# Low parts of x and xT of batches 1 to 7: subtracted on GpSimd instead of on the Vector engine

## The chip, the cores and the metric

One core of one Trainium2 chip runs the whole program. The metric is the device time of one execution in microseconds (us). Engines are named as the profile names them: PE is TensorE, DVE is VectorE, ACT is ScalarE, POOL is GpSimd, SP is SyncE, which here only issues DMAs.

## What is computed

Eight graphs (batches) of 1024 nodes with 256 features go through two graph layers, each with a residual and a layer norm:

```python
def layer0(x, adj, W):
    deg = jnp.sum(adj, axis=-1, keepdims=True)
    agg = jnp.einsum('bij,bjf->bif', adj, x) / jnp.maximum(deg, 1e-6)
    return relu(jnp.einsum('bnf,of->bno', jnp.concatenate([x, agg], axis=2), W))

def layer1(x, adj, k, bias):
    Ah = adj + eye
    dh = rsqrt(jnp.sum(Ah, axis=-1))
    An = dh[:, :, None] * Ah * dh[:, None, :]
    return relu(jnp.einsum('bnm,bmf,fc->bnc', An, x, k) + bias)

x = layernorm(x + layer0(x, adj, W))      # x: (8, 1024, 256), adj: (8, 1024, 1024)
x = layernorm(x + layer1(x, adj, k, bias))
```

## The kernel before

All values are float32. Before TensorE uses a matrix, the matrix is split in two: its high part is the value rounded to the matmul's format (`fp32r`), made by ACT with a copy, and its low part is the value minus the high part, made by DVE with a subtraction (`minus`, L443). A product is then three matmuls (L688 to L690): high by high, high by low, low by high. This holds for x (`x_hi`, `x_lo`), for its transpose, used in the projection of layer 0 (`xt_hi`, `xt_lo`), for the adjacency (`a_hi`, `a_lo`, tiles `adj_hi` and `adj_lo` in the profile), for the weights and for every intermediate that is multiplied again (`gath_hi`, `gath_lo`, `x1s_hi`, `x1s_lo`).

There is no scheduler. Each engine has its own program, written by hand and synchronised by counting semaphores, and batches 1 to 6 run in a loop on each engine. In the loop turn of batch b, PE does the second half of the adjacency-times-x product of b (`gather_second`), the projections of layer 0, the propagation of layer 1 (`propagate`), the projection of layer 1 (`project1`), and between those already the first half of the product of batch b+1 (`gather_first`). PE goes through one batch in this order:

- `propagate` for half 0 fills PSUM banks 0 and 1 of `ring_b`. ACT copies each bank to `gath_hi` and DVE makes `gath_lo` of it (`read_g`, numbers 0 and 1).
- `project1` for tiles 0 to 3 waits for `g_lo_done` of these two (L815), then come the rest of `propagate` and, from L820, `gather_first(b + 1, range(TH))`, which needs the first low parts of the new adjacency and of the new x.
- `project1` for tiles 4 to 7 waits for `g_lo_done` of `read_g` 2 and 3 (L821). Then `gather_first(b + 1, range(TH, T))` needs the second half of `x_lo`.
- `gather_second(b + 1, 0)` follows, then `project_x` for tiles 0 to 3, the first reader of `xt_lo` (L789); tiles 4 to 7 read its second piece (L796).

DVE's order in the same stretch (L600 to L625) is: the two halves of `x_lo` of b+1 (`split_x`), the two pieces of `xt_lo` of b+1 (`split_xt`), `read_g` 0 and 1, two chunks of `adj_lo`, `read_g` 2, two more chunks of `adj_lo`, `add_identity`, layer 1's bias, ReLU, residual and statistics (`add_layer1(b, 0)`), and only then `read_g` 3. ACT works through the matching list (L374 to L391), one step ahead of DVE.

POOL makes the identity matrix at the start and is idle afterwards. SP issues the load of the next batch's xT once `xt_lo_done` says that the present one has been split (L237); its next entry in the queue is the store of the first half of the output.

Batch 0's own splits are made in an opening section by DVE (L656 to L675, and L576 for one piece of xT).

Of the kernel before, what the change touches and what calls it, by code (L numbers as in the profile page):

```python
# [4 lines left out]
F32 = mybir.dt.float32  # L5
F32R = mybir.dt.float32r
ALU = mybir.AluOpType
# [3 lines left out]
B, N, F = 8, 1024, 256  # L11
T = N // P
FT = F // P
H = 2
# [6 lines left out]
XP = 2  # L21
# [8 lines left out]
def gnn_two_layers(nc, adjT, adjN, x, xT, w, k, bias, out):  # L30
# [8 lines left out]
    with ctx:  # L39
        def sb(name, shape, dt=F32, align=32):  # L40
            return ctx.enter_context(nc.sbuf_tensor(name, shape, dt, align_bytes=align))

        def sem(name):
            return ctx.enter_context(nc.semaphore(name))
# [4 lines left out]
        x_hi = sb("x_hi", [P, T, F], F32R, LINE)  # L49
        x_lo = sb("x_lo", [P, T, F], F32R, LINE)  # L50
        xt_hi = sb("xt_hi", [P, T, FT, P], F32R, LINE)
        xt_lo = sb("xt_lo", [P, T, FT, P], F32R, LINE)
# [4 lines left out]
        x_sb = sb("x_sb", [P, T, F])  # L57
        xt_raw = sb("xt_raw", [P, T, FT, P])
# [50 lines left out]
        x_hi_done, x_lo_done = sem("x_hi_done"), sem("x_lo_done")  # L109
        xt_hi_done, xt_lo_done = sem("xt_hi_done"), sem("xt_lo_done")  # L110
# [24 lines left out]
        def xt_pieces(t, first, end):  # L135
            return t[:, first * T // XP:end * T // XP, :, :].rearrange("p t f c -> p (t f c)")
# [7 lines left out]
        def x_half(t, h):  # L144
            return t[:, h * TH:(h + 1) * TH, :]
# [112 lines left out]
        def _(pool):  # L258
# [3 lines left out]
                                    fill=1.0, base=0, pattern=[[-1, P]],  # L262
                                    channel_multiplier=1).then_inc(ident_done, 1)

        @block.scalar
        def _(act):
            def copy(o, i):
# [174 lines left out]
        def _(dve):  # L442
            def minus(o, a, hi):  # L443
                return nc.vector.tensor_tensor(o, a, hi.bitcast(F32), ALU.subtract)  # L444
# [8 lines left out]
                                        ident[:, :, :].to_broadcast([P, TH, P]),  # L453
                                        ALU.add).then_inc(diag_ready, 1)

            def split_x(n, h):
                dve.wait_ge(x_hi_done, n * H + h + 1)
                minus(x_half(x_lo, h), x_half(x_sb, h), x_half(x_hi, h)).then_inc(x_lo_done, 1)

            def split_xt(n, i):  # L460
                dve.wait_ge(xt_hi_done, n * XP + i + 1)
                minus(xt_pieces(xt_lo, i, i + 1), xt_pieces(xt_raw, i, i + 1),
                      xt_pieces(xt_hi, i, i + 1)).then_inc(xt_lo_done, 1)

            def read_agg(b, n):
                dve.wait_ge(agg_hi_done, b * 4 + n + 1)
                minus(gath(gath_lo, n), ring_b[:, n, :], gath(gath_hi, n)).then_inc(agg_lo_done, 1)

            def read_g(b, n):
                dve.wait_ge(g_hi_done, b * 4 + n + 1)  # L470
                minus(gath(gath_lo, n), ring_b[:, n, :], gath(gath_hi, n)).then_inc(g_lo_done, 1)
# [6 lines left out]
            def inverse_degrees(b, h):  # L478
                half = b * H + h + 1
                dve.wait_ge(deg_done, b * T + TH * (h + 1))  # L480
                nc.vector.tensor_scalar(deg_c[:], deg[:, h * TH:(h + 1) * TH], DEG_EPS, None,
                                        ALU.max).then_inc(deg_clamped, 1)
                nc.vector.tensor_scalar(v[:, 0:TH], deg[:, h * TH:(h + 1) * TH], 1.0, None,
                                        ALU.add).then_inc(deg_read, 1)
                dve.wait_ge(deg_clamped, half)
                nc.vector.reciprocal(rdeg[:], deg_c[:]).then_inc(rdeg_done, 1)  # L486

            def add_layer0(b, h, pairs=range(0, TH, 2)):
                for q in pairs:
                    t = h * TH + q  # L490
                    for o in range(2):
                        dve.wait_ge(proj0_scaled, b * T + t + o + 1)
                        nc.vector.tensor_tensor(x1[:, t + o, :], ring_a[:, (t + o) % NB, 0:F],  # L493
                                                x1[:, t + o, :], ALU.add).then_inc(proj0_read, 1)
                    dve.wait_ge(proj0_read, b * T + t + 2)
                    nc.vector.scalar_tensor_tensor(
                        x1[:, t:t + 2, :], x1[:, t:t + 2, :], 0.0, x_sb[:, t:t + 2, :],
                        ALU.max, ALU.add).then_inc(resid0_done, 1)
                    dve.wait_ge(resid0_done, b * (T // 2) + t // 2 + 1)
                    for o in range(2):  # L500
                        last = nc.vector.bn_stats(stats[:, q + o, :], x1[:, t + o, :])
                    if q == TH - 2:
                        last.then_inc(stats_done, 1)
# [26 lines left out]
            def variances(b, step, at):  # L530
                n = b * 4 + step + 1
                even_mean, even_cv, odd_mean, odd_cv = (stats[:, :, i] for i in (1, 2, 4, 5))
                dve.wait_ge(stats_done, n)
                nc.vector.tensor_tensor(dmean[:], even_mean, odd_mean, ALU.subtract).then_inc(dmean_done, 1)
                nc.vector.tensor_tensor(smean[:], even_mean, odd_mean, ALU.add)
                nc.vector.scalar_tensor_tensor(cv[:], even_cv, F * LN_EPS, odd_cv, ALU.add, ALU.add)
                dve.wait_ge(dmean_done, n)
                nc.vector.scalar_tensor_tensor(dmean2[:], dmean[:], 0.25, dmean[:],
                                               ALU.mult, ALU.mult).then_inc(dmean2_done, 1)
                dve.wait_ge(dmean2_done, n)  # L540
                nc.vector.scalar_tensor_tensor(v[:, at:at + TH], cv[:], 1.0 / F, dmean2[:],  # L541
                                               ALU.mult, ALU.add).then_inc(var_ready, 1)
# [16 lines left out]
            def lower_x1s(b, h, tiles=range(TH)):  # L559
                for q in tiles:  # L560
                    t = h * TH + q
                    dve.wait_ge(x1s_hi_done, b * T + t + 1)
                    nc.vector.scalar_tensor_tensor(  # L563
                        x1s_lo[:, t, :], x1[:, t, :], dh[:, h, q:q + 1],
                        x1s_hi[:, t, :].bitcast(F32), ALU.mult, ALU.subtract).then_inc(x1s_lo_done, 1)
# [6 lines left out]
            def batch(b, more, first=False):  # L572
                inverse_degrees(b, 0)
                if first:
                    add_layer0(b, 0, [0])
                    split_xt(0, 1)  # L576
                    read_agg(b, 2)
                    add_layer0(b, 0, [2])
                else:
                    add_layer0(b, 0)  # L580
                variances(b, 0, TH)
                read_agg(b, 3 if first else 2)
                inverse_roots(b, 0, 2 * TH, dh[:, 0, :], dh[:, 0, TH:2 * TH])
                if not first:
                    read_agg(b, 3)
                lower_x1s(b, 0)
                inverse_degrees(b, 1)
                add_layer0(b, 1)
                variances(b, 1, TH)
                inverse_roots(b, 1, 2 * TH, dh[:, 1, :], dh[:, 1, TH:2 * TH])  # L590
                lower_x1s(b, 1)
                diagonal(b, 1)
                if first:
                    dve.wait_ge(k_hi_done, 1)
                    minus(k_lo[:], k_raw[:], k_hi[:]).then_inc(k_lo_done, 1)
                    dve.wait_ge(bias_loaded, 16)
                if not more:
                    finish(b)
                    return
                for h in range(H):  # L600
                    split_x(b + 1, h)
                for i in range(XP):
                    split_xt(b + 1, i)
                read_g(b, 0)
                read_g(b, 1)
                split_adj(b + 1, 0, 0)
                split_adj(b + 1, 0, 1)
                read_g(b, 2)
                split_adj(b + 1, 0, 2)
                split_adj(b + 1, 0, 3)  # L610
                add_identity(0)
                add_layer1(b, 0)
                read_g(b, 3)
                variances(b, 2, 0)
                split_adj(b + 1, 1, 0)
                inverse_roots(b, 2, TH, rstd1[:], rstd1[:])
                for i in range(1, CH):
                    split_adj(b + 1, 1, i)
                add_identity(1)
                add_layer1(b, 1)  # L620
                variances(b, 3, 0)
                read_agg(b + 1, 0)
                read_agg(b + 1, 1)
                inverse_roots(b, 3, TH, rstd1[:], rstd1[:])
                diagonal(b + 1, 0)  # L625
# [255 lines left out]
```

## Time and profile before

| | us |
|---|---|
| median of 3 runs | 506.6 (506.44 to 506.66) |
| the profiled execution | 506.57 |
| its span, first to last instruction | 504.8 |
| PE busy in the span | 491.4 (97%) |
| DVE busy | 393.8 (78%) |
| ACT busy | 327.8 (65%) |
| POOL busy | 0.7 |

The mean granted TensorE clock is 0.994 of full speed. The profiled execution is 1.8 us longer than its span, since a launch has some time around its first and last instruction, and it agrees with the median to 0.03 us. An engine's busy time says little here of what bounds the kernel: the views below show who waits for whom, and when.

### The profile page before, as it was taken

The page shows a single profiled execution, that of the slowest core. Times are in us where ns is not written, and L with a number is a line of the kernel's source. Part 1 is how long each engine was busy: PE and PEld are TensorE (multiplying, and loading weights), DVE is VectorE, ACT ScalarE, POOL GpSimd, SP SyncE. Part 2 cuts the span into 40 slices and gives each one's busy share as a digit, 9 for nine tenths or more (in the row PEclk, how much of TensorE's full clock was granted, in tenths as well). Part 3 has the DMA queues.
Part 4 walks back from the last instruction along what each step waited for, and adds up shares of the span by engine and source line. Part 5 has one row for each costly group of instructions (what it writes and reads, how often), then busy time and mean ns, then how long its engine had stood idle before and what let it go on. Part 6 is the DMA issues. An engine that isn't in the chain of part 4 may idle for free.

```text
span 504.8 us, 8135 instructions
## 1 busy us (share of the span) xinstructions
PE 491.4 (97%) x2750; PEld 430.7 (85%) x2750; DVE 393.8 (78%) x960; ACT 327.8 (65%) x601; POOL 0.7 (0%) x6
## 2 busy tenths in 40 slices
PE   7999999999999999999999999999999999999992
PEld 5988788988889888998889988898888988889992
DVE  4786898669966799667996679966898669976656
ACT  5795948757677657766586574955847757576422
POOL 0000000000000000000000000000000000000000
PEclk9999999999999999999999999999999999999997
DMA  7999517944097621955239361593607932061002
GB/s 259 409 373 359 208 48 251 374 120 174 6 349 270 201 90 66 369 188 208 83 117 396 113 211 77 200 385 82 246 1 258 366 115 93 0 208 43 1 0 83
DMA packets 26686, 93.38 MB, mean 185 GB/s; under 512 B 2864, under 2 KB 2992, under 8 KB 26672
## 3 DMA queue, kind: packets, MB, share of 16 engines
q1 hardware_dynamic: 26672, 93.20, 51.1%
q8 instruction: 8, 0.13, 0.1%
q14 instruction: 6, 0.05, 0.0%
HBM read 84.80 MB, written 8.39 MB: 185 GB/s over the span
## 4 chain that ended last, share of the span: by engine, by line
PE 96%; DVE 1%; DMA 1%; ACT 0%; issue 0%; ACTq 0%; SPq 0%
PE ring_b L688 23%; PE ring_b L690 23%; PE ring_b L689 23%; PE ring_a L688 9%; PE ring_a L690 9%; PE ring_a L689 9%; DMA adj_raw<-adjT 1%; DVE stats L521 0%; DVE x L513 0%; DVE u L509 0%; PE ring_b L721 0%; PE ring_b L729 0%; PE ring_b L725 0%; ACT adj_hi L268 0%; ACT x L333 0%
## 5 line engine op out<-in xcount | busy, mean ns | idle before, releaser
L688 PE MATMUL ring_b<-adj_hi,x_hi 128*128 128x512 f32 x254 | 99.4, 391 | 0.0
L689 PE MATMUL ring_b<-adj_lo,x_hi 128*128 128x512 f32 x254 | 99.0, 390 | 0.0
L690 PE MATMUL ring_b<-adj_hi,x_lo 128*128 128x512 f32 x254 | 99.0, 390 | 0.0
L688 PE MATMUL ring_b<-adj_hi,x1s_hi 128*128 128x512 f32 (+1 forms) x256 | 98.3, 384 | 0.0
L690 PE MATMUL ring_b<-adj_hi,x1s_lo 128*128 128x512 f32 (+1 forms) x256 | 98.0, 383 | 0.0
L689 PE MATMUL ring_b<-adj_lo,x1s_hi 128*128 128x512 f32 (+1 forms) x256 | 97.9, 382 | 0.0
L268 ACT ACTIVATE gath_hi<-ring_b 128x512 fp32r<-128x512 f32 (+1 forms) x64 | 36.6, 583 | 64.8 <-PE ring_b L690 64.7
L444 DVE TENSOR_TENSOR adj_lo<-adj_raw,adj_hi 128x1024 fp32r<-128x1024 f32 (+1 forms) x68 | 76.0, 1158 | 3.4 <-ACT adj_hi L268 3.4
L283 ACT ACTIVATE adj_nat<-adj_nat 128x1024 f32<-128x1024 f32 x64 | 67.1, 1052 | 5.0 <-DMA adj_nat<-adjN 4.9
L268 ACT ACTIVATE adj_hi<-adj_raw 128x1024 fp32r<-128x1024 f32 (+1 forms) x68 | 64.9, 999 | 0.8 <-DMA adj_raw<-adjT 0.6
L444 DVE TENSOR_TENSOR gath_lo<-ring_b,gath_hi 128x512 fp32r<-128x512 f32 (+1 forms) x64 | 42.7, 678 | 22.1 <-ACT gath_hi L268 22.1
L690 PEld LDWEIGHTS ring_b<-adj_hi,x_lo 128*128 128x128 f32 x254 | 47.8, 188 | 10.3
L690 PEld LDWEIGHTS ring_b<-adj_hi,x1s_lo 128*128 128x128 f32 x256 | 48.1, 188 | 9.8
L689 PEld LDWEIGHTS ring_b<-adj_lo,x_hi 128*128 128x128 f32 x254 | 47.8, 188 | 9.5
L688 PEld LDWEIGHTS ring_b<-adj_hi,x_hi 128*128 128x128 f32 x254 | 47.8, 188 | 9.5
L688 PEld LDWEIGHTS ring_b<-adj_hi,x1s_hi 128*128 128x128 f32 x256 | 48.1, 188 | 8.9 <-DVE x1s_lo L563 0.2
L689 PEld LDWEIGHTS ring_b<-adj_lo,x1s_hi 128*128 128x128 f32 x256 | 48.1, 188 | 8.9
L563 DVE SCALAR_TENSOR_TENSOR x1s_lo<-x,dh,x1s_hi 128x256 fp32r<-128x256 f32 x64 | 29.7, 484 | 32.0 <-ACT x1s_hi L317 32.0
L308 ACT ACTIVATE x<-ring_a,rdeg 128x256 f32<-128x256 f32 x64 | 27.4, 475 | 27.9 <-DVE rdeg L486 16.1
L300 ACT ACTIVATE rs_root<-rs_value 128x8 f32<-128x8 f32 (+1 forms) x32 | 6.5, 203 | 57.3 <-DVE rs_value L541 57.3
L322 ACT ACTIVATE x<-x,nb,dh 128x256 f32<-128x256 f32 x64 | 36.3, 592 | 9.4 <-DVE nb L556 9.4
L493 DVE TENSOR_TENSOR x<-ring_a,x 128x256 f32<-128x256 f32 x64 | 25.5, 419 | 20.0 <-ACT x L308 20.0
(87 smaller groups left out, 940.2 us busy)
## 6 DMA issues: line engine op xcount, KB each, us to landing
adj_nat<-adjN SPq DMA_DIRECT2D x64, 512.0 KB, 5.8
adj_raw<-adjT SPq DMA_DIRECT2D x60, 512.0 KB, 9.7
out<-x SPq DMA_DIRECT2D x15, 512.0 KB, 3.3
xt_raw<-xT SPq DMA_DIRECT2D x7, 1024.0 KB, 4.9
x_sb<-x SPq DMA_DIRECT2D x14, 512.0 KB, 5.1
adj_raw<-adjT SPq DMA_DIRECT2D x8, 256.0 KB, 6.4
x_sb<-x SPq DMA_DIRECT2D x4, 256.0 KB, 6.2
xt_raw<-xT SPq DMA_DIRECT2D x2, 512.0 KB, 12.0
```

Of the source, the lines that this page charges most:

```text
L268: return nc.scalar.activation(o, i, ACT.Copy)
L283: nc.scalar.activation(nat[:, t % NR, :], nat[:, t % NR, :], ACT.Copy, accum_out=deg[:, t:t + 1]).then_inc(deg_done, 1)
L300: nc.scalar.activation(s[:, 0:m], v[:, 0:m], ACT.Sqrt, scale=0.25).then_inc(root_done, 1)
L308: nc.scalar.activation(x1[:, t, :], ring_a[:, t % NB, F:2 * F], ACT.Copy, scale=rdeg[:, q:q + 1]).then_inc(proj0_scaled, 1)
L322: nc.scalar.activation(x1[:, t, :], x1[:, t, :], ACT.Identity, scale=dh[:, h, TH + q:TH + q + 1], bias=nb[:, q:q + 1]).then_inc(x1_done, 1)
L444: return nc.vector.tensor_tensor(o, a, hi.bitcast(F32), ALU.subtract)
L493: nc.vector.tensor_tensor(x1[:, t + o, :], ring_a[:, (t + o) % NB, 0:F], x1[:, t + o, :], ALU.add).then_inc(proj0_read, 1)
L563: nc.vector.scalar_tensor_tensor(x1s_lo[:, t, :], x1[:, t, :], dh[:, h, q:q + 1], x1s_hi[:, t, :].bitcast(F32), ALU.mult, ALU.subtract).th ...
L688: nc.tensor.matmul(o, lhi, rhi, start=(first and i == 0), stop=False)
L689: nc.tensor.matmul(o, lhi, rlo, start=False, stop=False)
L690: last = nc.tensor.matmul(o, llo, rhi, start=False, stop=last_part)
```

## The change

DVE's loop no longer contains the four subtractions that make `x_lo` and `xt_lo` of batch b+1. POOL gets a loop over batches 1 to 7 that makes them with the same operation, operands and shape, each after the same semaphore that DVE waited for, and each raising the same semaphore as before. Nothing else is edited. The opening section, for batch 0, still makes its low parts on DVE.

```diff
             nc.gpsimd.affine_select(...)
+
+            def minus(o, a, hi):
+                return nc.gpsimd.tensor_tensor(o, a, hi.bitcast(F32), ALU.subtract)
+
+            def split_x(n, h):
+                pool.wait_ge(x_hi_done, n * H + h + 1)
+                minus(x_half(x_lo, h), x_half(x_sb, h), x_half(x_hi, h)).then_inc(x_lo_done, 1)
+
+            def split_xt(n, i):
+                pool.wait_ge(xt_hi_done, n * XP + i + 1)
+                minus(xt_pieces(xt_lo, i, i + 1), xt_pieces(xt_raw, i, i + 1),
+                      xt_pieces(xt_hi, i, i + 1)).then_inc(xt_lo_done, 1)
+
+            pool.wait_ge(x_lo_done, H)
+            pool.wait_ge(xt_lo_done, XP)
+            with pool.Fori(1, B) as n:
+                for h in range(H):
+                    split_x(n, h)
+                for i in range(XP):
+                    split_xt(n, i)
...
-            def split_x(n, h):
-                dve.wait_ge(x_hi_done, n * H + h + 1)
-                minus(x_half(x_lo, h), x_half(x_sb, h), x_half(x_hi, h)).then_inc(x_lo_done, 1)
-
...
-                for h in range(H):
-                    split_x(b + 1, h)
-                for i in range(XP):
-                    split_xt(b + 1, i)
                 read_g(b, 0)
                 read_g(b, 1)
                 split_adj(b + 1, 0, 0)
```

On DVE, at the end of batch 0 (the loop's batches are alike, without `k_lo`), the program before has these instructions in a row; `u` is a scratch tile, `ring_a` and `ring_b` are PSUM, all other names are tiles in SBUF:

```order
L444 TENSOR_TENSOR adj_lo<-adj_diag,adj_hi 128x4x128
L444 TENSOR_TENSOR k_lo<-u,k_hi 128x512
L444 TENSOR_TENSOR x_lo<-x_sb,x_hi 128x1024 x2
L444 TENSOR_TENSOR xt_lo<-xt_raw,xt_hi 128x1024 x2
L444 TENSOR_TENSOR gath_lo<-ring_b,gath_hi 128x512 x2
L444 TENSOR_TENSOR adj_lo<-adj_raw,adj_hi 128x1024 x2
L444 TENSOR_TENSOR gath_lo<-ring_b,gath_hi 128x512
```

The changed program has the following in the same place. The two rows with `x_lo` and `xt_lo` are gone and what stood behind them has moved up; its order is the same:

```order
L464 TENSOR_TENSOR adj_lo<-adj_diag,adj_hi 128x4x128
L464 TENSOR_TENSOR k_lo<-u,k_hi 128x512
L464 TENSOR_TENSOR gath_lo<-ring_b,gath_hi 128x512 x2
L464 TENSOR_TENSOR adj_lo<-adj_raw,adj_hi 128x1024 x2
L464 TENSOR_TENSOR gath_lo<-ring_b,gath_hi 128x512
```

On POOL the changed program has this behind the identity matrix, from the loop's first row to its branch; the program before has nothing there:

```order
L279 ISA
L266 ISA
L266 TENSOR_TENSOR x_lo<-x_sb,x_hi 128x1024
L269 REGISTER_ALU
L266 TENSOR_TENSOR x_lo<-x_sb,x_hi 128x1024
L266 TENSOR_TENSOR xt_lo<-xt_raw,xt_hi 128x1024 x2
L279 REGISTER_ALU
L279 COMPARE_AND_BRANCH
```

The two ISA rows are register arithmetic and a selection of POOL's instruction library. Both stand ahead of the wait for x, so they run when the turn before has ended.

## Rows read from the trace of the kernel before

**Rows 1.** Waits of PE, longest and shortest of three: us in total, times, longest us.

```profile
PE ring_b L721 <- ACT adj_hi L268: 2.5, 1, 2.5
...
PE ring_a L688 <- issue: 0.3, 1, 0.3
```

**Rows 2.** One batch: start:end, length, busy PE, PEld, DVE, ACT, POOL, granted clock, DMA.

```profile
242.00:302.64 60.64, 60.64 (x338) 53.02 (x337) 48.66 (x119) 40.42 (x75) 0.00 (x0) 1.00 0.54 191
```

**Rows 3.** DVE in order of time, us 295 to 314 (start, length, what, idle before).

```profile
295.61 0.69 DVE L444 TENSOR_TENSOR adj_lo<-adj_diag,adj_hi 128x512 fp32r<-128x512 f32 x1
296.22 2.35 DVE L444 TENSOR_TENSOR x_lo<-x_sb,x_hi 128x1024 fp32r<-128x1024 f32 x2
298.49 2.35 DVE L444 TENSOR_TENSOR xt_lo<-xt_raw,xt_hi 128x1024 fp32r<-128x1024 f32 x2
...
302.10 0.69 DVE L444 TENSOR_TENSOR gath_lo<-ring_b,gath_hi 128x512 fp32r<-128x512 f32 x1 [0.66 <-ACT gath_hi L268]
303.05 2.36 DVE L444 TENSOR_TENSOR adj_lo<-adj_raw,adj_hi 128x1024 fp32r<-128x1024 f32 x2 [0.26 <-ACT adj_hi L268]
305.32 0.68 DVE L444 TENSOR_TENSOR gath_lo<-ring_b,gath_hi 128x512 fp32r<-128x512 f32 x1
305.92 2.35 DVE L444 TENSOR_TENSOR adj_lo<-adj_raw,adj_hi 128x1024 fp32r<-128x1024 f32 x2
...
313.39 0.67 DVE L444 TENSOR_TENSOR gath_lo<-ring_b,gath_hi 128x512 fp32r<-128x512 f32 x1
```

**Rows 4.** ACT in order of time, us 295 to 304.

```profile
295.08 1.99 ACT L268 ACTIVATE x_hi<-x_sb 128x1024 fp32r<-128x1024 f32 x2
296.98 1.99 ACT L268 ACTIVATE xt_hi<-xt_raw 128x1024 fp32r<-128x1024 f32 x2
...
301.96 2.00 ACT L268 ACTIVATE adj_hi<-adj_raw 128x1024 fp32r<-128x1024 f32 x2
```

**Rows 5.** PE in order of time, us 303 to 340: the first matmul behind each wait.

```profile
303.99 0.28 PE L688 MATMUL ring_a<-k_hi,gath_hi 128*128 128x256 f32 x1
...
309.57 0.39 PE L688 MATMUL ring_b<-adj_hi,x_hi 128*128 128x512 f32 x1
...
315.01 0.28 PE L688 MATMUL ring_a<-k_hi,gath_hi 128*128 128x256 f32 x1
...
328.76 0.28 PE L688 MATMUL ring_a<-w_hi,xt_hi 128*128 128x256 f32 x1
```

**Rows 6.** Batch 0: DVE in order of time, us 54 to 73.

```profile
54.95 0.68 DVE L444 TENSOR_TENSOR k_lo<-u,k_hi 128x512 fp32r<-128x512 f32 x1
...
60.09 1.28 DVE L444 TENSOR_TENSOR gath_lo<-ring_b,gath_hi 128x512 fp32r<-128x512 f32 x2
61.29 2.35 DVE L444 TENSOR_TENSOR adj_lo<-adj_raw,adj_hi 128x1024 fp32r<-128x1024 f32 x2
...
64.16 2.35 DVE L444 TENSOR_TENSOR adj_lo<-adj_raw,adj_hi 128x1024 fp32r<-128x1024 f32 x2
...
71.62 0.67 DVE L444 TENSOR_TENSOR gath_lo<-ring_b,gath_hi 128x512 fp32r<-128x512 f32 x1
```

**Rows 7.** Batch 0: PE in order of time, the two `project1` starts.

```profile
61.48 0.36 PE L688 MATMUL ring_a<-k_hi,gath_hi 128*128 128x256 f32 x1 [0.29 <-issue]
...
72.47 0.28 PE L688 MATMUL ring_a<-k_hi,gath_hi 128*128 128x256 f32 x1
```

**Rows 8.** Batch 0: ACT in order of time, the new adjacency's first two chunks.

```profile
59.00 2.00 ACT L268 ACTIVATE adj_hi<-adj_raw 128x1024 fp32r<-128x1024 f32 x2
```

**Rows 9.** POOL's instructions by line: xcount, busy us, mean ns, idle before.

```profile
L261 POOL TENSOR_SCALAR_AFFINE_SELECT ident<-ident 128x128 f32<-128x128 f32 x1 | 0.3, 294 | 0.2 <-POOL ident L259 0.2
L259 POOL MEMSET ident<- 128x128 f32 x1 | 0.2, 205 | 0.3 <-POOLq L875 0.3
L875 POOL MEMSET const-bfloat16-1.0<- 128x1 bf16 x1 | 0.1, 102 | 0.0
```

**Rows 10.** SP's queue in order of time: the load of xT for the next batch.

```profile
301.03 0.38 SPq L238 DMA_DIRECT2D xt_raw<-xT  x1
```

## The prediction, made before the changed kernel was timed

> **What bounds the kernel now.** I read the waits of PE first, since PE is busy in 97% of the span. The list has three entries in all, the longest of 2.5 us before the first matmuls of the program, and the last, of 0.3 us, in batch 0 [rows 1]. In the loop PE never waits: over one period of 60.64 us it is busy for 60.64 us at a granted clock of 1.00, while DVE is busy for 48.66 us and ACT for 40.42 us [rows 2]. So the loop is bound by PE's own matmuls. DVE's work is hidden, and a shorter DVE list gives nothing unless PE waits for it somewhere. It follows that the change can gain almost nothing, and the question is whether it makes PE wait.
>
> For that I looked for the tightest hand-overs from DVE to PE, in the stretch that the change touches. In order of time, DVE makes the four low parts at 296.2 to 300.8 us, and then waits 0.66 us for ACT, which itself has to wait for PE, before `gath_lo` number 1, and 0.26 us for ACT again before the first `adj_lo` chunk at 303.05 [rows 3]. From there it runs without a gap up to `gath_lo` number 3, which ends at 313.39 + 0.67 = 314.06. PE's `project1` for tile 4, which waits for it, starts at 315.01 [rows 5]. How much of this 0.95 us is really spare is shown by batch 0, where PE did wait: `gath_lo` number 1 ended at 60.09 + 1.28 = 61.37 [rows 6] and the matmul began at 61.48 [rows 7], 0.11 us later. So **the slack is 0.84 us** in batches 1 to 6. In batch 0 the same hand-over has `gath_lo` at 71.62 + 0.67 = 72.29 [rows 6] and the matmul at 72.47 [rows 7], less 0.11: a slack of 0.07 us.
>
> **What is removed.** Four subtractions of 128x1024 leave DVE in each of seven turns. Two of them take 2.35 us in a row [rows 3], and starts are 1.135 us apart (305.92 - 303.05, less 0.60 from the start of `gath_lo` 2 at 305.32 to 305.92, is 2.27 for two), so 4.5 us of DVE go per batch. In batches 1 to 6 nothing moves forward for it. `gath_lo` 0 can start early, but `gath_lo` 1 and the first `adj_lo` are gated by ACT, as the idle times before them show [rows 3], and ACT's copies are gated by PE. The chain of 11 us that decides the slack still begins at 303.05. The 4.5 us become idle time of DVE ahead of it. In batch 0, `gath_lo` 1 no longer comes late, which gives PE its 0.29 us back [rows 7], and the chain can begin when ACT's first chunk is ready, 59.00 + 1.0 = 60.0 [rows 8], and not at 61.29 [rows 6]. Gain of this part: 0.3 us in all.
>
> **What is added: the length of a POOL subtraction.** No row shows one. POOL's memset of 128 columns takes 205 ns and one of 1 column 102 ns, which is 0.81 ns a column for writing. The affine select, with one input, takes 294 ns, which is (294 - 102)/127 = 1.51 ns a column [rows 9]. So reading one operand costs 0.70 ns on top of writing. A second operand at the same price gives 2.21 ns a column, or 0.10 + 1024 x 2.21 = **2.36 us**. The lower bound is a second operand for nothing, 0.10 + 1024 x 1.51 = 1.65 us. The upper is a second operand at the price of the whole select, 3.02 ns a column and 3.2 us. I take 2.36, since it charges both reads alike. The Trainium skill, in GPSIMD Engine Reference, section 3.1, gives 4497 ns for this operation at 2048 columns and 2293 ns for DVE, and tells one to keep elementwise work on DVE. Half of that would be an estimate of 2.25 us, no row here shows it, and the sum of the next part would fall by about 3 us with it.
>
> **When POOL works.** `x_hi` is ready from 295.08 + 1.0, and all four high parts by 296.98 + 1.99 = 298.97 [rows 4], so only the first one is waited for. DVE's diagonal ends at 295.61 + 0.69 = 296.30 [rows 3]. Four subtractions from 296.30 end at 298.66, 301.02, 303.38 and 305.74, where DVE was done at 300.8. Their direct readers don't mind: PE first uses `x_lo` at 309.57 and `xt_lo` at 328.76 [rows 5], 11 and 25 us after they are written. SP issues the next load of xT, at 301.03 before [rows 10], about 5 us later; its next entry, the store, comes 18 us later, and the data is needed one batch later, so this costs nothing. The ISA row in POOL's loop runs ahead of the wait, in 50 us of idle POOL; before the affine select the same kind of row left 0.2 us idle [rows 9].
>
> **What lies beside it.** DVE's stream from 303.05 overlaps with POOL by 305.74 - 303.05 = 2.69 us. Its first four `adj_lo` chunks and `add_identity` take two operands from SBUF, as POOL's subtraction does; `gath_lo` takes one from PSUM. The trace has no DVE instruction beside a POOL instruction with inputs. The cost is therefore bounded from both sides: nothing, if both run at their own pace, as ACT and DVE do in [rows 3, 4]; or the whole overlap, if a POOL instruction and a DVE instruction with two SBUF operands exclude each other. Below nothing it cannot be, as DVE's chain starts no earlier in the loop. I take exclusion. Both engines do the same two-operand work on the same memory in the same microsecond, and a division of one path in equal shares would cost DVE the same total, because the same operands have to pass it. The Trainium skill, SBUF — State Buffer, section "Who interferes with whom", says that a DVE instruction with two SBUF inputs and a GpSimd one that reads SBUF contend for one shared interface, and that the second to start blocks fully. No row of this case shows it.
>
> The sum depends on who is next when both are ready:
>
> - **By turns.** The third POOL instruction holds until 303.38, `adj_lo` 0 runs to 304.51, POOL's fourth to 306.87, `adj_lo` 1 to 308.00, `gath_lo` 2 to 308.60. `adj_lo` 2 starts at 308.60 where it was 305.92, so the chain is 2.68 us late. Less the slack, PE waits 2.68 - 0.84 = 1.84 us. Six batches: 11.0 us. In batch 0, POOL starts near 55.0 and takes turns with `k_lo` too (57.4 to 58.0), then runs 58.0 to 60.4, and with `adj_lo` 0 and 1 in between to 63.9 and, after 65.0, to 67.4, where `adj_lo` 2 started at 64.16: 3.2 us late, 3.1 after the slack. Sum 14.1, or 506.6 + 14.1 = 520.7 us.
> - **DVE keeps its place** while it has such work. After 303.38 both `adj_lo` run to 305.65, POOL's fourth takes 305.65 to 308.01, and `gath_lo` 2 runs beside it. `adj_lo` 2 starts at 308.01, 2.09 late, so PE waits 1.25 us, 7.5 in six. By the same steps batch 0 costs 2.2. Sum 9.7, or 516.3 us.
>
> I take the middle, **518.5 us**. The time of POOL's instruction counts three times over: with 2.1 us by turns the loop's wait is 0.81 and the sum is 514.2, with 2.6 us it is 2.81 and 527.5. Once PE waits, the delay does not grow from batch to batch, because ACT's next copies are released by PE and wait with it.
>
> **Rivals.**
>
> - **No measurable change.** POOL and DVE don't hinder each other, or POOL needs 1.65 us: its last instruction then ends at 302.9, before DVE's chain. PE waits nowhere in the loop, batch 0 lies between -0.3 and +0.9 us, and the time is 506.3 to 507.5. For it speaks that ACT and DVE share SBUF without a mark; against it, that the slack is under 1 us and that a sharing of any size that costs DVE more than 0.84 of its 11 us breaks it. Chance 0.13.
> - **Faster.** The one place where PE waits for DVE's list is the 0.29 us in batch 0 [rows 7]; the point from which it decides is 1 us, so the four instructions would also have to shorten a hand-over that no row shows as a wait. The time would be 505.4 or less. Chance 0.03.
> - **A weak interference**, in which DVE loses less than half of the overlap: 1.1 us late, 0.3 us of PE per batch and 1 in batch 0, about 509 us. Chance 0.12, and it is slower too.
> - **Slow POOL.** At 3.2 us an instruction, the third ends at 305.9 and the fourth, by turns, runs from 307.0 to 310.2. `adj_lo` 2 starts at about 311.9, 6 us late, and PE waits 5.1 us a batch. With batch 0 it is about 543 us. Chance of 527 or more: 0.04.
> - That the change does not do what it says: the order of the two programs shows the four rows gone from DVE and present on POOL, so it does.
>
> **How the numbers follow.** Exclusion, or an equal share, with POOL at 2.1 to 2.6 us has 0.68, between 512 and 527 us. With the weak case that makes 0.80 for a range of **508 to 527 us**; left out are no change or faster (0.16) and the slow POOL (0.04). A measurement of this kernel can tell 0.2%, 1.0 us, from no change. Faster by more 0.03, within 0.13, slower by more 0.84. The sums were made against the profiled execution of 506.57 us, whose span is 504.8; the median is 506.6, so no correction is due.
>
> **What the profile of the changed kernel would show.** PE has a new wait, for DVE's `gath_lo`, once in each of seven batches, before `project1` of tile 4, of 1.2 to 1.9 us in the loop and 2 to 3 in batch 0; the period grows from 60.64 to about 62.2 us. POOL has 28 subtractions near 2.4 us, from 296.3 on. DVE is idle at 296 to 299, and its `adj_lo` rows near 303 are stretched, or follow an idle time, by 2 to 2.7 us in sum. DVE's busy time falls by some 30 us and that gives PE nothing. I am wrong if the `adj_lo` rows keep their 1.13 us beside a busy POOL; if POOL's instructions are outside 2.1 to 2.6 us, which moves the sum by about 2.6 us for each 0.1 us; or if PE waits at another place, `gath_lo` 1 above all, whose own slack is 303.99 - 0.11 - (302.10 + 0.69) = 1.09 us [rows 3, 5].

## The result, and the profile after

The changed kernel takes **520.25 us** (median of 4 runs, 520.15 to 520.42) against 506.56 us for the kernel before, measured with it: 1.027 times the time, 95% interval 1.0256 to 1.0281. The prediction was 518.5 us in a range of 508 to 527, and its step "by turns" gave 520.7.

The first view is what PE waits for, as in [rows 1]: line waited for, us in total, times, longest us.

```profile
PE ring_a L700 <- DVE gath_lo L464: 11.0, 7, 2.8
PE ring_b L733 <- ACT adj_hi L288: 2.6, 1, 2.6
PE ring_a L728 <- DVE x1s_hi L664: 1.2, 1, 1.2
```

One wait is new, and it is the one that the prediction named: seven times, once per batch that POOL works for, for `gath_lo`. The short entry of 0.3 us in batch 0 is gone. One turn of the loop, the row that answers to [rows 2] (start:end, length, busy PE, PEld, DVE, ACT, POOL, granted clock, DMA):

```profile
249.30:311.57 62.27, 60.91 (x338) 52.94 (x337) 46.46 (x115) 40.34 (x75) 10.48 (x5) 1.00 0.50 185
```

The period has grown from 60.64 to 62.27 us, by 1.63. DVE is 2.2 us less busy than before although 4.5 us of work were taken from it, so what is left takes longer. Where it does is seen in order of time. POOL, from 305 us:

```profile
305.04 4.77 POOL L266 TENSOR_TENSOR x_lo<-x_sb,x_hi 128x1024 fp32r<-128x1024 f32 x2 [51.79 <-ACT x_hi L288]
309.77 5.75 POOL L266 TENSOR_TENSOR xt_lo<-xt_raw,xt_hi 128x1024 fp32r<-128x1024 f32 x2
```

and DVE, the rows that answer to [rows 3]:

```profile
304.44 0.69 DVE L464 TENSOR_TENSOR adj_lo<-adj_diag,adj_hi 128x512 fp32r<-128x512 f32 x1
308.31 0.69 DVE L464 TENSOR_TENSOR gath_lo<-ring_b,gath_hi 128x512 fp32r<-128x512 f32 x1 [3.18 <-ACT gath_hi L288]
310.94 0.69 DVE L464 TENSOR_TENSOR gath_lo<-ring_b,gath_hi 128x512 fp32r<-128x512 f32 x1 [1.94 <-ACT gath_hi L288]
311.89 4.71 DVE L464 TENSOR_TENSOR adj_lo<-adj_raw,adj_hi 128x1024 fp32r<-128x1024 f32 x2 [0.26 <-ACT adj_hi L288]
316.52 0.68 DVE L464 TENSOR_TENSOR gath_lo<-ring_b,gath_hi 128x512 fp32r<-128x512 f32 x1
317.12 2.34 DVE L464 TENSOR_TENSOR adj_lo<-adj_raw,adj_hi 128x1024 fp32r<-128x1024 f32 x2
...
324.58 0.67 DVE L464 TENSOR_TENSOR gath_lo<-ring_b,gath_hi 128x512 fp32r<-128x512 f32 x1
```

The freed time is the idle time of 3.18 and 1.94 us before the two `gath_lo`. The pair of `adj_lo` that took 2.36 us takes 4.71, and everything behind it keeps its old length: the chain is 2.36 us late at `gath_lo` 2. The two `gath_lo`, which stand beside POOL's second and third instructions, take 0.69 us as before, and these two instructions of POOL take 2.40 us each. A narrower stretch of the same views shows the turns one by one:

```profile
309.77 2.40 POOL L266 TENSOR_TENSOR xt_lo<-xt_raw,xt_hi 128x1024 fp32r<-128x1024 f32 x1
```

```profile
311.89 1.36 DVE L464 TENSOR_TENSOR adj_lo<-adj_raw,adj_hi 128x1024 fp32r<-128x1024 f32 x1 [0.26 <-ACT adj_hi L288]
```

```profile
313.17 3.43 DVE L464 TENSOR_TENSOR adj_lo<-adj_raw,adj_hi 128x1024 fp32r<-128x1024 f32 x1
```

```profile
312.13 3.39 POOL L266 TENSOR_TENSOR xt_lo<-xt_raw,xt_hi 128x1024 fp32r<-128x1024 f32 x1
```

DVE's first `adj_lo` is stretched by 0.14 us until POOL's third instruction ends. POOL's fourth starts at 312.13 and takes 3.39 us, 1.0 more than its own 2.40, while DVE finishes that `adj_lo`. It ends at 315.52, and DVE's second `adj_lo`, which has waited for it inside its 3.43 us, ends 1.08 us later, at 316.60. The time spent waiting stands inside the recorded length of the instructions and in no list of waits. At the end of the chain PE starts `project1` for tile 4, answering to the third row of [rows 5]:

```profile
323.63 0.39 PE L702 MATMUL ring_b<-adj_hi,x_lo 128*128 128x512 f32 x1
325.39 0.38 PE L700 MATMUL ring_a<-k_hi,gath_hi 128*128 128x256 f32 x1 [1.37 <-DVE gath_lo L464]
```

The list of waits is a little short here. The matmul before the stop is recorded with 0.39 us, but in a row without stops the next one starts 0.23 us after it (314.79 and 315.01 at this place in the kernel before). The two starts above are 1.76 us apart, so PE was held for 1.53 us, 0.16 more than the 1.37 of the list. The same 0.16 us is missing from every listed wait behind such a matmul.

In batch 0 the same wait is 2.83 us long, and something else follows it. The stretches are the wait and the 3.4 us behind it:

```profile
72.00:74.80 2.80, 0.00 (x0) 0.00 (x0) 2.73 (x8) 0.00 (x0) 0.00 (x0) 1.00 0.00 0
74.80:78.20 3.40, 3.40 (x16) 3.40 (x17) 3.23 (x12) 2.92 (x4) 0.00 (x0) 0.52 0.00 0
```

The granted clock is 0.52 there, the lower of its two levels (1.2 GHz and not 2.4): 16 matmuls are 0.213 us apart instead of 0.118, which is 1.5 us more. So the 13.7 us between the spans (518.5 and 504.8) are six loop turns of 1.63, 9.8 us, and batch 0 with the rest, 3.9: `project1` of tile 4 starts at 74.80 and not 72.47, 2.3 us, and the clock costs 1.5.

### The profile page after: what moved, and what is told of

Its sections match the earlier page's. It is cut to its first block, busy times and chain, and to the rows that moved or that the text cites. A ratio compares the mean times of both kernels' runs of the same rounds, so it can differ in the third digit from the quotient of the medians.

```text
span 518.5 us, 8173 instructions
## 1 busy us (share of the span) xinstructions
PE 494.3 (95%) x2750; PEld 431.8 (83%) x2750; DVE 380.3 (73%) x932; ACT 327.7 (63%) x601; POOL 75.6 (15%) x34
## 4 chain that ended last, share of the span: by engine, by line
PE 76%; DVE 14%; issue 5%; ACT 2%; DMA 1%; ACTq 0%; DVEq 0%; SPq 0%
PE ring_b L700 17%; PE ring_b L702 17%; PE ring_b L701 17%; PE ring_a L700 8%; PE ring_a L702 8%; PE ring_a L701 8%; DVE adj_lo L464 5%; DVE u L525 2%; DVE x L529 2%; DVE stats L537 2%; DVE gath_lo L464 2%; ACT adj_hi L288 1%; DMA adj_raw<-adjT 1%; DVE adj_diag L472 1%; ACT gath_hi L288 1%
## 5 line engine op out<-in xcount | busy, mean ns | idle before, releaser
L464 DVE TENSOR_TENSOR adj_lo<-adj_raw,adj_hi 128x1024 fp32r<-128x1024 f32 (+1 forms) x68 | 94.0, 1421 | 4.2 <-ACT adj_hi L288 4.1
L266 POOL TENSOR_TENSOR x_lo<-x_sb,x_hi 128x1024 fp32r<-128x1024 f32 x14 | 33.9, 2446 | 363.7 <-ACT x_hi L288 363.7
L303 ACT ACTIVATE adj_nat<-adj_nat 128x1024 f32<-128x1024 f32 x64 | 67.1, 1052 | 5.3 <-DMA adj_nat<-adjN 5.0
L700 PE MATMUL ring_a<-k_hi,gath_hi 128*128 128x256 f32 x120 | 35.2, 293 | 11.0 <-DVE gath_lo L464 11.0
```

The source lines that it names most:

```text
L266: return nc.gpsimd.tensor_tensor(o, a, hi.bitcast(F32), ALU.subtract)
L303: nc.scalar.activation(nat[:, t % NR, :], nat[:, t % NR, :], ACT.Copy, accum_out=deg[:, t:t + 1]).then_inc(deg_done, 1)
L700: nc.tensor.matmul(o, lhi, rhi, start=(first and i == 0), stop=False)
```

## The experiments

The theory (A): a POOL instruction that reads SBUF and a DVE instruction with two SBUF operands exclude each other and take turns, and PE pays for what exceeds the slack of the first hand-over behind it. Rivals: a POOL subtraction has one price wherever it stands (B); the late `xt_lo` is what costs (C). The opening section of the program ends up to 2 us earlier or later from one run to another (the first `x_lo` on POOL starts at 54.06 us in the profile of e6, at 54.73 in that of the changed kernel and at 55.94 in that of e5), so I read the loop's period first and the total second. The kernel before, run beside them, had medians of 506.59 to 506.66 us.

| kernel | what differs from the changed kernel | period, us | time, us |
|---|---|---|---|
| before | | 60.64 | 506.6 |
| changed | | 62.27 | 520.25 |
| e1 | POOL makes `xt_lo` only | 60.64 | 507.3 |
| e8 | POOL makes `x_lo` only | 61.0 | 511.5 |
| e3 | memsets in place of `xt_lo` | 60.64 | 505.9 |
| e7 | one-input instructions in place of `xt_lo` | 66.1 and 67.1 in turn | 550.0 |
| e4 | not for batch 1 | 62.3 | 516.2 |
| e5 | `xt_lo` in half instructions | 61.8 | 517.6 |
| e6 | `gath_lo` 3 earlier | 61.7 | 514.9 |
| e9 | e6, and `gath_lo` 0 and 1 earlier | 61.1 to 61.7, mean 61.4 | 511.2 |
| e10 | e9's order, nothing on POOL | 60.64 | 506.6 |
| e11 | changed kernel once more | 62.3 | 521.5 |

**e1: half of the instructions, the ones that look late.**

```diff
 (POOL)         with pool.Fori(1, B) as n:
-                for h in range(H):
-                    split_x(n, h)
                 for i in range(XP):
                     split_xt(n, i)
 (DVE)
+                for h in range(H):
+                    split_x(b + 1, h)
                 read_g(b, 0)
```

> POOL makes only xt_lo; x_lo goes back to DVE. Theory A (a POOL subtraction and a DVE instruction with two SBUF operands exclude each other and take turns; PE pays what exceeds its 0.84 us of slack): in the loop DVE's x_lo ends near 298.6 on the clock of the kernel before, POOL's two instructions of 2.4 us end near 303.4, so the first adj_lo is held up by 0.3 to 0.4 us, less than the slack, and PE does not wait in the loop. Only batch 0, with almost no slack, pays 1 to 2 us: 507.5 to 508.5 us. Rival B (each POOL subtraction costs the same wherever it stands, half of 13.7 us for half of the instructions): 513.4 us. Rival C (the late xt_lo, or the later load of xT behind it, is what costs): 518 to 520 us, as xt_lo is still late.

Measured 507.3 us, 1.0018 times before (1.0002 to 1.0034), 0.2 us under what was expected. In the loop the `adj_lo` pair is back at its length and PE does not wait:

```profile
299.63 5.09 POOL L266 TENSOR_TENSOR xt_lo<-xt_raw,xt_hi 128x1024 fp32r<-128x1024 f32 x2 [55.56 <-ACT xt_hi L285]
```

```profile
304.57 2.36 DVE L461 TENSOR_TENSOR adj_lo<-adj_raw,adj_hi 128x1024 fp32r<-128x1024 f32 x2 [0.26 <-ACT adj_hi L285]
```

POOL ends at 304.72, when DVE has just asked. In batch 0, where the two still overlap, PE waits once, 1.2 us. B falls: half of the instructions do not cost half. C is only weakened by this run, since its `xt_lo` is done 0.15 us after the first `adj_lo` has started and that of the changed kernel 3.63 us after. What settles C is e3 below: there `xt_lo` is done 3.78 us after, and PE does not wait.

**e8: the other half.**

```diff
 (POOL)             for h in range(H):
                     split_x(n, h)
-                for i in range(XP):
-                    split_xt(n, i)
 (DVE)
+                for i in range(XP):
+                    split_xt(b + 1, i)
                 read_g(b, 0)
```

> The mirror image of e1: POOL makes x_lo, DVE xt_lo. Theory A with turns: POOL's two instructions now stand beside DVE's two subtractions of xT, which queue ahead of gath_lo 0 and 1; gath_lo 1 ends 0.6 us later than PE can use it, so PE waits at project1 of tile 0 in each batch and no longer at tile 4: 0.8 us a batch with the refill, 5 in the loop and 2 to 4 in batch 0, 513.5 to 515.5 us, with the same number of POOL instructions as e1, which cost 0.7 us. Rival B (each POOL subtraction has one price): as e1, 507.3 us.

Measured 511.5 us, 1.0089 (1.0066 to 1.0112). It is dearer than e1 with the same number of POOL instructions, and the wait moved from tile 4 to tile 0 as expected. The size was missed: 0.4 us a batch and not 0.8, 511.5 us and not 513.5 to 515.5. DVE's row shows the turns: its pair of `xt_lo`, 2.35 us when alone, takes 4.98, of which 1.64 is the first.

```profile
302.20 4.98 DVE L461 TENSOR_TENSOR xt_lo<-xt_raw,xt_hi 128x1024 fp32r<-128x1024 f32 x2 [1.75 <-ACT xt_hi L285]
307.11 1.28 DVE L461 TENSOR_TENSOR gath_lo<-ring_b,gath_hi 128x512 fp32r<-128x512 f32 x2
```

```profile
307.92 0.39 PE L701 MATMUL ring_b<-adj_hi,x1s_lo 128*128 128x512 f32 x1
308.48 0.35 PE L699 MATMUL ring_a<-k_hi,gath_hi 128*128 128x256 f32 x1 [0.18 <-issue]
```

PE's matmul at tile 0 starts 0.09 us after `gath_lo` 1 ends, at 308.39. The list gives a wait of 0.18 us, but the starts are 0.56 us apart instead of 0.23, so PE was held for 0.33 us. A delay of 0.6 us had been expected.

**e3: POOL busy without reading.** The three memsets per piece leave out the low part of xT.

```diff
-                minus(xt_pieces(xt_lo, i, i + 1), ...)
+                for k in range(3):
+                    last = nc.gpsimd.memset(xt_pieces(xt_lo, i, i + 1).bitcast(F32), 0.0)
+                    if k < 2:
+                        last.then_inc(wrote, 1)
+                        pool.wait_ge(wrote, 4 * (n - 1) + 2 * i + k + 1)
+                last.then_inc(xt_lo_done, 1)
...
-            with pool.Fori(1, B) as n:
+            for n in range(1, B):
```

> POOL still makes x_lo by subtraction, but each piece of xt_lo is now three memsets (the low part of xT is left out and is zero), which read nothing from SBUF, and POOL's loop is unrolled. POOL stays busy from about 301 to 307 beside the adj_lo chain, longer than with the subtractions. Theory A in the narrow form (it is POOL's reading that excludes DVE's second SBUF operand): adj_lo keeps 1.2 us, PE does not wait in the loop, 506.3 to 507.5 us. Rival D (any busy POOL blocks DVE, writing too): at least as slow as the changed kernel, 520 us or more.

Measured 505.9 us, 0.9993 (0.9979 to 1.0007), 0.4 us under what was expected. POOL is busy from 300.1 to 306.0 us, and DVE's pair beside it keeps its length:

```profile
300.10 5.90 POOL L276 MEMSET xt_lo<- 128x1024 f32 x6
```

```profile
302.22 2.36 DVE L469 TENSOR_TENSOR adj_lo<-adj_raw,adj_hi 128x1024 fp32r<-128x1024 f32 x2 [0.26 <-ACT adj_hi L293]
```

So it is not POOL's being busy, nor its writing, that stops DVE (rival D falls). POOL's last write of `xt_lo` ends at 306.00, as late behind the first `adj_lo` as in the changed kernel, so a late `xt_lo` does not cost anything either (C falls).

**e7: POOL reads one operand.** The low part of xT is replaced here by 1e-8 times xT, made twice over all 2048 columns, and the second half of `x_lo` waits for `xt_hi` too, which leaves POOL idle for 0.42 us.

```diff
-                for i in range(XP):
-                    split_xt(n, i)
+                for k in range(2):
+                    last = nc.gpsimd.tensor_scalar(xt_pieces(xt_lo, 0, XP), xt_pieces(xt_raw, 0, XP),
+                                                   1e-8, None, ALU.mult)
```

> The low part of xT is replaced by 1e-8 times xT, made by POOL with an instruction of one input over all 2048 columns, twice. Theory A in the narrow form (a POOL instruction that reads SBUF at all excludes DVE's second operand): one adj_lo of DVE is stretched by most of the length of a POOL instruction, 1.9 to 3.3 us, as with the two-input subtraction; PE waits in the loop. Rival H (only POOL instructions with two inputs contend): adj_lo keeps 1.2 us and PE does not wait, 506 to 507.5 us.

Measured once: 550.0 us. PE has seven waits, 28.2 us in all, and the granted clock is 0.50 to 0.52 for some 3.4 us behind each of them. `adj_lo` is stretched in both pairs, so one operand read by POOL is enough (rival H falls).

```profile
193.97 5.38 POOL L285 TENSOR_SCALAR xt_lo<-xt_raw 128x2048 fp32r<-128x2048 f32 x1
199.51 5.55 POOL L285 TENSOR_SCALAR xt_lo<-xt_raw 128x2048 fp32r<-128x2048 f32 x1 [0.15 <-POOL xt_lo L285]
```

```profile
195.61 4.22 DVE L471 TENSOR_TENSOR adj_lo<-adj_raw,adj_hi 128x1024 fp32r<-128x1024 f32 x2 [0.26 <-ACT adj_hi L295]
199.75 0.68 DVE L471 TENSOR_TENSOR gath_lo<-ring_b,gath_hi 128x512 fp32r<-128x512 f32 x1
200.35 5.19 DVE L471 TENSOR_TENSOR adj_lo<-adj_raw,adj_hi 128x1024 fp32r<-128x1024 f32 x2
```

DVE's first pair ends at 199.83. Its first instruction went on at about 197.6, although POOL's record ends at 199.35. What POOL does in the 1.7 us between stays open.

**e4: batch 0's turn as before.**

```diff
 (POOL)
-            with pool.Fori(1, B) as n:
+            with pool.Fori(2, B) as n:
 (DVE)
+                if first:
+                    for h in range(H):
+                        split_x(b + 1, h)
+                    for i in range(XP):
+                        split_xt(b + 1, i)
```

> The change for batches 2 to 7 alone; the low parts of batch 1, made during batch 0, stay on DVE. Theory A with the loop's part as read from the trace, six times 1.63 us, and nothing in batch 0: 506.6 + 9.8 = 516.4 us, PE with six waits of 1.4 us and a granted clock of 1.00 behind each of them; the 3.9 us of batch 0 (2.4 of waiting and 1.5 of 16 matmuls at the lower clock level) are gone. Rival E (the fall of the clock in batch 0 belongs to the place or to chance, not to the wait of 2.8 us): it shows again and the time is about 518 us.

Measured 516.2 us; 516.4 was expected. PE has six waits, 8.4 us in all, the longest 1.4, and the granted clock behind each of the six is 1.00. Six turns of 1.63 us and batch 0's 3.9 us are shown apart by it. Of rival E, the part that the fall of the clock belongs to the place falls: the place is the same and the long stop is gone. That chance has a share in it is not excluded, as e5 and e11 show.

**e5: shorter POOL instructions.**

```diff
-                minus(xt_pieces(xt_lo, i, i + 1), ...)
+                for k in range(2):
+                    cols = slice(k * 512, (k + 1) * 512)
+                    last = minus(xt_pieces(xt_lo, i, i + 1)[:, cols], ...)
```

> POOL makes each piece of xt_lo in two instructions of 512 columns, same work in all. Theory A with turns between single instructions: each instruction of POOL takes about 1.2 us, the last one stands beside gath_lo 2, which does not contend, for 0.6 us of its time, so adj_lo number 2 is 2.1 us late and not 2.36, PE's waits are shorter by 0.26 us: the sum is about 518.6 us, or down to 517 where batch 0 then keeps its clock. Rival G (DVE shares the path in proportion, or POOL keeps it until its queue is empty): 520 us as in the changed kernel.

Measured 517.6 us, within what was expected, with PE waits of 0.9 us in the loop where 1.1 was forecast from 1.37. DVE's single `adj_lo` is now stretched to 2.32 us, by one POOL instruction of half the length:

```profile
249.79 2.32 DVE L467 TENSOR_TENSOR adj_lo<-adj_raw,adj_hi 128x1024 fp32r<-128x1024 f32 x1
```

The turn is taken between single instructions, not between queues (rival G falls).

**e6: more slack at the hand-over.** From here on the POOL part of the change is complete and only DVE's order differs.

```diff
-                add_layer1(b, 0)
-                read_g(b, 3)
+                add_pair(b, 0, 0)
+                stats_pair(b, 0, 0)
+                read_g(b, 3)
+                add_pair(b, 0, 2)
+                stats_pair(b, 0, 2)
```

> The whole change, but DVE makes gath_lo number 3 between the first and the second pair of tiles of add_layer1, which takes about 2.2 us of other work from in front of it: the slack of the hand-over grows from 0.84 to about 3.1 us. Theory A: DVE's adj_lo rows are stretched by the same 2.3 us as in the changed kernel, but PE does not wait in the loop; batch 0 pays at most 0.5 us: 506.4 to 507.2 us. Rivals B and C (the cost does not hang on this hand-over): 515 to 520 us.

Measured 514.9 us: **my expectation was wrong by 8 us**. The time lies at the edge of what B and C would give, but e1 had ruled them out, and the trace has another answer. The wait at tile 4 is gone in the loop (batch 0 keeps 0.54 us) and a shorter one has appeared at another place, the first `project_x` of the next batch:

```profile
149.02 0.38 PE L703 MATMUL ring_a<-w_hi,xt_hi 128*128 128x256 f32 x1 [0.82 <-DVE gath_lo L464]
```

That matmul waits for `gath_lo` 0 and 1 of the new batch, as the code requires before `project_x` (`agg_lo_done`). In the kernel before, the same two rows of DVE and PE are these:

```profile
265.16 1.29 DVE L444 TENSOR_TENSOR gath_lo<-ring_b,gath_hi 128x512 fp32r<-128x512 f32 x2
```

```profile
268.12 0.28 PE L688 MATMUL ring_a<-w_hi,xt_hi 128*128 128x256 f32 x1
```

The pair ends at 266.45 us and the matmul starts at 268.12, a slack of 1.56 after the same 0.11. DVE waits for nobody between the two hand-overs, so it carries its delay from one to the next. In e6 this pair starts 25.28 us after the first `adj_lo` (122.32 and 147.60), where the kernel before has 22.75 (242.41 and 265.16): 2.53 us late. Less the slack that is 0.97 us, and PE was held for 0.98: its matmul starts 1.21 us after the one before, at 147.81, instead of 0.23. In the changed kernel this was hidden, since PE had already stopped for 1.4 us ahead of it.

**e9: slack at both.**

```diff
-                add_layer1(b, 1)
-                variances(b, 3, 0)
-                read_agg(b + 1, 0)
-                read_agg(b + 1, 1)
+                add_pair(b, 1, 0)
+                stats_pair(b, 1, 0)
+                add_pair(b, 1, 2)
+                read_agg(b + 1, 0)
+                read_agg(b + 1, 1)
+                stats_pair(b, 1, 2)
+                variances(b, 3, 0)
```

> e6 showed that with a wider first hand-over DVE's delay of 2.36 us reaches PE at the next one, gath_lo 0 and 1 of the new batch before project_x, whose slack is 1.56 us: a wait of 0.82 us. Here DVE also makes these two ahead of the last statistics and the variances of the half before, 1.3 us earlier, so that slack grows to about 2.9 us. Theory A (only slack against a delay of 2.4 us counts): no wait of PE in the loop at either place, adj_lo stretched as before, batch 0 pays 0.5 to 1 us: 506.6 to 507.6 us. Rival F (there is always a next hand-over, DVE as a whole is the bound once it shares its operands' path): again 510 us or more.

Measured 511.2 us: better than e6, but not the 506.6 to 507.6 that were expected. The second wait is gone from the list, though not from the kernel. The matmul there still starts 0.14 us after `gath_lo` 0 and 1 end (209.88), and 0.39 us after the one before it:

```profile
209.63 0.39 PE L708 MATMUL ring_b<-adj_hi,x_lo 128*128 128x512 f32 x1
210.02 0.38 PE L706 MATMUL ring_a<-w_hi,xt_hi 128*128 128x256 f32 x1
```

PE is held here for 0.15 to 0.25 us in every batch. The first wait is back with 0.2 to 0.5 us in five of the six turns. DVE's rows show why:

```profile
244.08 0.69 DVE L464 TENSOR_TENSOR gath_lo<-ring_b,gath_hi 128x512 fp32r<-128x512 f32 x1 [0.58 <-ACT gath_hi L288]
245.03 6.08 DVE L464 TENSOR_TENSOR adj_lo<-adj_raw,adj_hi 128x1024 fp32r<-128x1024 f32 x2 [0.26 <-ACT adj_hi L288]
```

The pair takes 6.08 us, 1.4 more than in the changed kernel. There POOL began 6.85 us before the first `adj_lo`; here it begins at 239.54, 5.49 us before it, so more of POOL's work meets DVE's. The head start and the length of the pair sum to 11.57 us here, to 11.56 in the changed kernel and to 11.57 to 11.60 in the other five turns of e9: each microsecond by which POOL starts later makes the pair longer by as much. DVE's delay has travelled through the whole batch, by way of the layer norm that DVE and ACT make in turn, to the `x_hi` that POOL waits for. This is the row of ACT through which it passes, and from its end to `x_hi` at 238.41 ACT only waits for DVE's part of the same norm and works:

```profile
233.51 0.21 ACT L320 ACTIVATE rs_root<-rs_value 128x8 f32<-128x8 f32 x1 [3.54 <-DVE rs_value L557]
```

The stops of PE take the delay back. The one turn in which PE had no listed wait (0.11 us held) is followed by a pair of 6.08 us and a wait of 0.45. So rival F was right in its first half, that there is a next hand-over, and in its 510 us or more. Its second half, that DVE as a whole is the bound, is not shown: DVE is idle for 3.19 us before `gath_lo` 0 in this turn.

**e10: the new order alone.** The kernel before with the two edits of e6 and e9.

> Control for e6 and e9: the kernel before, all subtractions on DVE, with the two changes of DVE's order that e9 has and nothing on POOL. If the order costs nothing by itself, PE waits nowhere in the loop, the period stays 60.64 us and the time is 506.4 to 507 us; then what e9 lost over the kernel before is due to POOL's instructions. If the new order is to blame (rival F: the later variances make the chain behind them late enough for PE), PE waits here too, 1 us or more in all.

Measured 506.6 us, 1.0001 (0.9988 to 1.0015), period 60.64 us, no wait of PE in the loop. The order is not to blame for e9: here DVE's `x_lo` starts 6.82 us ahead of the first `adj_lo` (297.06 and 303.88), as in the kernel before.

**e11: the changed kernel again.**

> The changed kernel once more, unaltered, to see whether the fall of TensorE's clock behind the wait of 2.8 us in batch 0 comes back. Expected if it belongs to that wait: the granted clock is about 0.5 for 3.4 us from 75 us on, 16 matmuls are 0.22 us apart, 520.0 to 520.6 us. In e5 a wait of 2.77 us at the same place left the clock at 1.00; if the same happens here the time is about 518.8 us.

Measured 521.5 us (520.4 to 521.7), some 1 us above what was expected: in the profiled execution the opening section ends 1.0 us later (`x_lo` on POOL at 55.69 and not 54.73), and the six turns of 62.30 us add 0.2. The wait of batch 0 is 2.80 us and ends at 75.76. The clock is lower behind it again, but not at once: 12 matmuls run at 1.00 first.

```profile
75.76:77.26 1.50, 1.50 (x12) 1.50 (x13) 1.47 (x7) 1.03 (x2) 0.00 (x0) 1.00 0.00 0
77.28:80.70 3.42, 3.42 (x17) 3.23 (x16) 3.28 (x9) 3.42 (x7) 0.00 (x0) 0.50 0.00 0
```

The fall came back, and its place relative to the stop did not.

## Why the prediction was right, point by point

- **Where PE has slack.** Right. The hand-over at `gath_lo` 3 is where PE waits, seven times. 0.84 us was a good value: the delay of 2.36 us less 0.84 is 1.52, and by the starts PE was held for 1.53 (the list has 1.37). The period is longer by 1.63, since the first matmul after the stop is followed by the next after 0.22 us and not 0.12.
- **Nothing gained by the removal.** Right: the 4.5 us became idle time before `gath_lo` 0 and 1.
- **POOL's length.** 2.36 us forecast, 2.40 measured when undisturbed, 2.37 from start to start. The way to it was weaker than the result: it charged the second operand 0.7 ns a column on top of one-input work, and in e7 one-input work held DVE off for some 3.6 us on 2048 columns, 1.75 ns a column, where the affine select's row had given 1.51.
- **Exclusion, by turns.** Right, and shown by more than the total: e3 (no reading, no cost), e7 (one input is enough), e5 (the turn is one instruction long), the untouched `gath_lo` with a PSUM operand, and the constant sum of head start and pair in e9. The rule of the Trainium skill cited in the prediction (SBUF — State Buffer, section "Who interferes with whom") agrees with these rows on who contends, and the order of turns is what they add. The delay by turns was forecast as 2.68 us and was 2.36; the 1.84 us of PE were 1.63. The mis-sized term is the way from the start of the first `adj_lo` to that of `gath_lo` 2, 4.95 us forecast and 4.63 measured. Of the 0.32 us, 0.18 is the place of the overlap: POOL began 6.85 us ahead of the first `adj_lo`, not 6.75, and DVE waited 0.14 us for the third instruction and not 0.33. The other 0.14 lies behind it: from the second `adj_lo` to `gath_lo` 2 it is 3.35 us, where one POOL instruction and one of DVE had been taken at 2.36 + 1.13 = 3.49. The middle of the two orders, which I took, was further off than the first order alone. That this order came within 0.5 us of the time is partly luck: it had 11.0 us in the loop, where 9.8 were measured, and 3.1 in batch 0, where 3.9 were, and the two errors offset each other.
- **Batch 0.** 3.1 us forecast, 3.9 measured, and right for another reason. The waiting was less: `k_lo` went first and kept its 0.68 us, and POOL's first instruction waited for it (2.95 us), where I had POOL go first. `project1` of tile 4 came 2.3 us later, not 3.1. The clock's 1.5 us was no term of the sum. I had not asked what a stop of PE costs besides its length.
- **DVE's busy time.** Wrong: a fall of some 30 us was forecast, and it fell by 13.5 (393.8 to 380.3), because the waiting is recorded as part of DVE's instructions.
- **The delay does not grow.** True of the changed kernel, for the reason given. As e6 and e9 show, it holds only because PE stops at the first hand-over. The prediction spoke of the slack of one hand-over; the kernel has several in a row, 0.84 and 1.56 us, and a way round through ACT and the layer norm.

No version with the subtractions on POOL beat the kernel before. e3's 0.7 us is within its interval.

## What to carry to other kernels

Before work is moved to an idle engine, ask what that engine shares with the one relieved, and look at what stands beside the moved work in time, not at the busy shares: here fourteen of the same instructions cost 0.7 us in e1 and 4.9 us in e8, according to what DVE did beside them. A relieved engine that was not the bound gives nothing, while a delay on it is charged at the tightest hand-over, and where that is widened, at the next. If POOL must do such work, place it beside DVE instructions with an operand from PSUM, or let it be work that only writes.

## What the runs showed of the hardware

- A POOL instruction that reads SBUF, with one input or two, and a DVE instruction with two SBUF operands exclude each other, one instruction at a time and in turns. This is seen with three tiles of DVE: `adj_lo`, `xt_lo` in e8, and `k_lo` in batch 0. A DVE instruction with one operand from PSUM (0.69 us) and a POOL memset (0.96 us for 1024 columns) are not concerned. The waiting stands in the recorded length: 3.43 us for a DVE subtraction of 1.22, 3.39 for one of POOL of 2.40.
- TensorE's clock, which stood at 1.00 before, was at its lower level for 3.4 us right behind a stop of 2.83 us in one run, and for 3.4 us again in e11, there from 1.5 us after the end of a stop of 2.80 us. It stayed at 1.00 behind stops of 2.77 (e5), 2.49 (e8) and 1.37 us. What decides between 2.77 and 2.80 us, and when the fall comes, is open; the three come from one profiled execution each. In e7 the clock was at 0.50 to 0.52 behind all seven stops, one of 5.88 us and six of 3.71; behind the first of these six:

```profile
144.20:147.50 3.30, 3.28 (x15) 3.29 (x16) 3.13 (x11) 2.89 (x4) 0.00 (x0) 0.50 0.02 5
```

In the changed kernel the stop of 2.83 us cost about half as much again.
